# Projections: DMA queue order in the first, second and last batch, earlier mask rows, and one row product moved

## Chip, cores and metric

The kernel runs on one core of a Trainium2 chip. The metric is the device time of one execution in microseconds (us). An execution taken by the hardware profiler gives the trace that is read here. In it PE is TensorE (PEld its weight loads), DVE is VectorE, ACT is ScalarE, POOL is GpSimd and SP is SyncE, which here only issues DMAs.

## The reference, cut to what matters

A cross-attention block and a feed-forward block, 8 batches of 512 tokens with 512 features, 16 heads. The part that the change touches is the projection of queries, keys and values and what it prepares.

```python
q = split_heads(layernorm(x) @ Wq.T + bq)
k = split_heads(ctx @ Wk.T + bk)
v = split_heads(ctx @ Wv.T + bv)
scores = einsum('bhqd,bhkd->bhqk', q, k) / sqrt(32)
scores = where(mask == 0, -1e9, scores) + attn_bias
x = x + (einsum('bhqk,bhkd->bhqd', softmax(scores), v)) @ Wo.T + bo
x = x + feed_forward(layernorm(x))     # W1, gelu, W2, and a routed low-rank part
```

## The kernel before

The kernel has three blocks in a row: `project` makes q, k and v of all batches and stores them in DRAM, `attend` does the attention, `blend` the output projection and the feed-forward part. All engines end a block before the next begins. Within a block each engine runs a program of its own, written out by hand in `walk(engine, body)`, with one `body(b, more)` for each batch b; semaphores order them. So on each engine, and on SP's DMA queue, an instruction that waits holds all that stand behind it.

All products are of 32-bit numbers split into a high and a low half, three passes for each (`PASSES`). PE, for each batch: four key products (L797 on), four value products, four query products, of 12 matmuls with 512 columns each; each product ends in one of four PSUM banks of `ps_j`, which ACT (keys, `k_s`) or DVE (values `v_s`, queries `q_s`) must have evicted before the bank's next product starts. Between them stand the row products (`row_product`, L719): DVE makes diagonal matrices (`diagonal`, L501 on) of a per-token factor, and one matmul with ones turns them into a row over the tokens. R_HIGH and R_LOW are the two halves of 1/std of x; they are summed in one bank. FAC is 1 for a query row that has any allowed key. They stand after the first value product (R_HIGH), after the second or third (R_LOW), and at the end of the values (FAC); in batch 0 FAC stands behind the last query product. `keep_row` (L658) copies the R row on ACT, L692 the FAC row; DVE multiplies the queries by both (`scale_queries`, `mask_queries`).

DVE's order in a batch (L549 on): statistics of x, high half of 1/std with its diagonals, low half of xT (`p_xT_l`, L572), diagonals of R_LOW, first value tile, then the mask rows (L587 to L596): `pos` from the mask, its minimum over keys, and `q_fac` from it; the diagonals of FAC, the other values, the low half of the next context (`context_low`, L498), the queries. POOL makes 1/std (`root`, L435), four sums of a piece of the feed-forward weight W1 (`weight_sums`, L422 on) and the low halves of seven operands of it (L458). ACT makes the high halves (`feed_high`, L650), which wait for the load of the piece (`wf_in`) and for the sums. ACT does the piece of batch b at the end of batch b, that of batch 0 in batch 1. In the last batch POOL also makes three mask tiles for the attention (L405, L411, L417; 128x2048 each); the second waits for its bias load and for the last `p_xT_l`.

SP's queue (L314 to L367) in a batch: load the W1 piece (`load_ff`), next context, next x, store keys, next xT, store pos, next mask, store values, store queries, wait for `wf_low`, store the feed parts (`store_ff`, two DMAs of 896 KB). In batch 0 the two halves of Wo (`store_wo`, 1 MB each) and the W1 piece go out between mask and values. In the last batch the four query tiles are stored one by one; before the third SP waits for the feed parts, loads `late.pos` and stores the feed parts.

Of the kernel before, what the change touches and what calls it, by code (L numbers as in the profile page):

```python
# [20 lines left out]
I32 = mybir.dt.int32  # L21
ALU = mybir.AluOpType
ACT = mybir.ActivationFunctionType
AX_X = mybir.AxisListType.X
# [6 lines left out]
NC = D // P  # L31
# [9 lines left out]
MASKED = 1.0e9  # L41
# [83 lines left out]
def tokens(ap):  # L125

    return ap.rearrange("(t p) n -> p t n", p=P)
# [32 lines left out]
def project(nc, ident, ones, neg_half, x, xT, ctxT, mask, WqT, bq, WkT, bk, WvT, bv, W1T,  # L160
# [3 lines left out]
    with ExitStack() as ctx:  # L164
# [9 lines left out]
        c_raw, m_raw, pos = late.bias  # L174
# [5 lines left out]
        pos_min = sb("pos_min", [P, NT])  # L180
# [70 lines left out]
        def _(sp):  # L251
# [23 lines left out]
            def store_qk(b, src, dst, out):  # L275
                sp.dma_start(dst.rearrange("(c b) p n -> b p c n", c=NC)[b], src[:, :, :]).then_inc(out, 16)
# [10 lines left out]
            def store_wo():  # L287
                for n, part in enumerate((wf_h, wf_l)):
                    sp.dma_start(wo_d[n], part[:, :, :, :].rearrange("p f i n -> p (f i n)").bitcast(F32)) \
                        .then_inc(wo_out, 16)  # L290
# [21 lines left out]
                        sp.dma_start(ahead.k[:, n, :], k_d[n]).then_inc(ahead.qk_in[n], 16)  # L312

            def body(b, more):  # L314
                if b > 0:
                    sp.wait_ge(wf_low, 4 * b)
                    load_ff(b)
                if not more:
                    sp.wait_ge(cT_low, B - 1)
                    load_bias(1)  # L320
                if b >= B - 3:
                    load_ahead(b - (B - 3))
                if more:
                    need(sp, cT_low, b)
                    if b == 0:
                        sp.wait_ge(piece_low, 2 * NC)
                    load_c(b + 1)
                    sp.wait_ge(stats_done, NT * (b + 1))
                    load_x(b + 1)
                sp.wait_ge(k_done, NC * (b + 1))  # L330
                store_qk(b, k_s, k_d, k_out)
                if more:
                    sp.wait_ge(xT_low, NC * (b + 1))
                    load_xT(b + 1)
                sp.wait_ge(pos_done, b + 1)
                sp.dma_start(tokens(pos_d[b]), pos[:, :, :]).then_inc(pos_out, 16)
                if more:
                    load_m(b + 1)
                else:
                    load_bias(2)  # L340
                if b == 0:
                    sp.wait_ge(wo_low, 1)
                    store_wo()
                    load_ff(b)
                for t in range(0 if more else NT):
                    sp.wait_ge(bank_free, NPB + NVQ * b + t + 1)
                    sp.dma_start(tokens(v_d[b])[:, t, :], v_s[:, t, :]).then_inc(v_out, 16)
                    if t == 1:
                        sp.wait_ge(min_done, B)
                        sp.wait_ge(pos_out, 16 * (B + 1))  # L350
                        load_bias(3)
                sp.wait_ge(bank_free, NPB + NVQ * b + NT)
                if more:
                    sp.dma_start(tokens(v_d[b]), v_s[:, :, :]).then_inc(v_out, 16)
                if more:
                    sp.wait_ge(q_done, NC * (b + 1))
                    store_qk(b, q_s, q_d, q_out)
                else:
                    for c in range(NC):
                        if c == NC // 2:  # L360
                            load_more_pos()
                            store_ff(b)
                        sp.wait_ge(q_done, NC * b + c + 1)
                        sp.dma_start(q_d[B * c + b], q_s[:, c, :]).then_inc(q_out, 16)
                if more:
                    sp.wait_ge(wf_low, 4 * b + 4)
                    store_ff(b)  # L367

# [97 lines left out]
        def _(dve):  # L466
# [72 lines left out]
            def first_minima(j):  # L539
                for i in range(HG):  # L540
# [4 lines left out]
                                             late.tiles[j][:, i:i + 1, :], 1.0, 3.0e38, ALU.add, ALU.min,  # L545
                                             late.nmax[:, j, i:i + 1]).then_inc(late.summed, 1)

            def body(b, more):

                dve.wait_ge(x_in, 16 * b + 16)  # L550
# [16 lines left out]
                if b == 0:  # L567
                    weight_low(0)
                    add_weights()
                for c in range(NC):  # L570
                    dve.wait_ge(xT_high, NC * b + c + 1)
                    dve.tensor_tensor(out=xT_l[:, c, :], in0=xT_raw[:, c, :], in1=xT_h[:, c, :].bitcast(F32),  # L572
                                      op=ALU.subtract).then_inc(xT_low, 1)
# [7 lines left out]
                if b == 0:  # L581
# [2 lines left out]
                    values(b, 1, NT)  # L584
                    dve.wait_ge(w_low, 2 * NC)

                dve.wait_ge(m_in, 16 * b + 16)  # L587
                dve.wait_ge(pos_out, 16 * (b + 1))
                dve.tensor_scalar(pos[:, :, :], m_raw[:, :, :].bitcast(I32), 0.0, MASKED, ALU.is_equal, ALU.mult) \
                    .then_inc(pos_done, 1)  # L590
                dve.wait_ge(pos_done, b + 1)
                dve.tensor_reduce(pos_min[:, :], pos[:, :, :], AX_X, ALU.min).then_inc(min_done, 1)
                dve.wait_ge(min_done, b + 1)


                dve.tensor_scalar(q_fac[:, :], pos_min[:, :], 0.0, None, ALU.is_equal).then_inc(fac_done, 1)  # L596
                dve.wait_ge(fac_done, NFAC * b + FAC)
                dve.wait_ge(fac_turned, NFAC * b + R_LOW)
                diagonal(q_fac)
# [114 lines left out]
        def _(pe):  # L714
# [51 lines left out]
            def body(b, more):  # L766
# [14 lines left out]
                def features(w, a, c):  # L781
                    cs = slice(c * P, (c + 1) * P)
                    return [(w[m][:, k, cs], a[n][:, k, :]) for k in range(NC) for m, n in PASSES]

                need(pe, cT_low, b)
                if b == 0:
                    first_keys()
                else:
                    for c in range(NC):
                        product(K_AT + c, features((w_h[1], w_l[1]), (cT_h, cT_l), c))  # L790
                for t in range(NT):
                    ts = slice(t * P, (t + 1) * P)
                    product(V_AT + t, [(a[:, k, ts], w[:, k, :]) for k in range(NC)
                                       for a, w in ((cT_h, w_h[2]), (cT_h, w_l[2]), (cT_l, w_h[2]))])
                    if t == 0:
                        row_product(b, R_HIGH)
                    if b == 0 and t == 1:  # L797
                        weight_means()
                    if t == (1 if b else 2):
                        row_product(b, R_LOW)  # L800
                if b > 0:
                    row_product(b, FAC)
# [1 line left out]
                pe.wait_ge(xT_low, NC * (b + 1))  # L804
                for c in range(NC):
                    product(Q_AT + c, features((w_h[0], w_l[0]), (xT_h, xT_l), c))
                    if b == 0 and c == NC - 1:
                        row_product(b, FAC)
                    if not more and c == 0:
                        pe.wait_ge(ahead.qk_in[0], 32)  # L810
                        pe.wait_ge(fac_row_done, 2 * B)
                        scores(0)
                    if not more and c == 2:
                        pe.wait_ge(late.summed, HG)
                        scores(1)
# [1396 lines left out]
```

## Time and profile before

| | |
|---|---|
| median of 3 runs | 1797.74 us (1796.21 to 1799.68) |
| the profiled execution | 1796.49 us, span 1794.7 us |
| projections / attention from | 0 / about 299.7 us |
| PE busy over the span | 1763.7 us (98%) |
| DVE, ACT, POOL busy | 1271.9, 912.4, 972.3 us |
| chain that ended last | PE 50% (L2126 20%, L2100 17%, L1999 7%, L2038 5%), DVE 2% |
| DMA | 396.90 MB, mean 221 GB/s |

The time between the span and the execution is 1.8 us. PE's busy time is modelled and its instructions overlap, so that a full PE shows as 98%; what the projections lose has to be read from the timeline, instruction by instruction. A row of the timeline names start, duration, engine, line, operation, tiles, the number of merged instructions, and in brackets the idle time before it with what released it. An engine that waits inside an instruction (for a memory port) shows as busy.

### The profile page before, as it was taken

Reading aid. Unit: us, or ns where it says so; the run is one execution under the profiler, and the core shown is the slowest. Engines: PE = TensorE matmul, PEld = TensorE weight load, DVE = VectorE, ACT = ScalarE, POOL = GpSimd, SP = SyncE. Lnnn points to the kernel's source line nnn. Section 1 sums busy time; section 2 is a strip of 40 time slices with the busy share of each in tenths; the row PEclk is TensorE's granted clock in tenths of the full one; section 3 lists DMA queues with packets and bytes.
Section 4 is the critical chain, followed back from the end, with each engine's and each line's share of the span. In section 5 each row is a group of like instructions: output and inputs, shape, how many; then the busy total and the mean of one; then the engine's idle time right before and its main releaser. Section 6 shows DMA issues by size and latency. Waiting matters only on the chain.

```text
span 1794.7 us, 33910 instructions
## 1 busy us (share of the span) xinstructions
PE 1763.7 (98%) x11842; PEld 1359.1 (76%) x11842; DVE 1271.9 (71%) x2866; ACT 912.4 (51%) x2038; POOL 972.3 (54%) x466
## 2 busy tenths in 40 slices
PE   9899998999999999999999999999999999999999
PEld 7688885555555555555788888888988889888888
DVE  7677777999999999999757565455654556645553
ACT  4222324999999999999534242312423224222231
POOL 1423336999999999999446333233342333423321
PEclk9999998999999999999999999999999999999999
DMA  9799999636437245430479694865948669577584
GB/s 320 285 372 341 341 357 314 224 114 217 129 109 235 95 142 195 136 131 13 154 246 308 211 311 131 314 201 180 323 136 294 212 192 311 164 254 246 164 277 146
DMA packets 213079, 396.90 MB, mean 221 GB/s; under 512 B 15280, under 2 KB 54832, under 8 KB 212400
## 3 DMA queue, kind: packets, MB, share of 16 engines
q1 hardware_dynamic: 209360, 381.62, 63.2%
q0 software_dynamic: 3264, 12.58, 2.0%
q8 instruction: 98, 1.61, 0.4%
q10 hardware_dynamic: 288, 0.52, 0.1%
q14 instruction: 69, 0.57, 0.1%
HBM read 319.17 MB, written 75.50 MB: 220 GB/s over the span
## 4 chain that ended last, share of the span: by engine, by line
PE 50%; DVE 2%; issue 0%; POOL 0%; ACT 0%; DVEq 0%; ACTq 0%
PE banks L2126 20%; PE banks L2100 17%; PE banks L1999 7%; PE banks L2038 5%; PE banks L1993 1%; DVE k_x L1554 0%; DVE k_x L1725 0%; DVE h_q L1715 0%; DVE n_w L1652 0%; DVE n_ru_l L1540 0%; DVE n_stats L1561 0%; DVE n_zo L1547 0%; DVE n_sel L1660 0%; DVE n_g_h L1732 0%; DVE k_az L1577 0%
## 5 line engine op out<-in xcount | busy, mean ns | idle before, releaser
L2100 PEld LDWEIGHTS banks<-n_zo,n_w 128*128 128x128 f32 x2688 | 500.2, 188 | 66.3 <-DVE h_bias L1838 2.4
L2100 PE MATMUL banks<-n_zo,n_w 128*128 128x256 f32 x2688 | 533.4, 282 | 3.5 <-DVE h_bias L1838 2.2
L1483 POOL TENSOR_TENSOR n_g_l<-h_pos,n_g_h 128x512 fp32r<-128x512 f32 x128 | 196.2, 1533 | 558.9 <-DVE n_g_h L1732 558.9
L2126 PE MATMUL banks<-n_w,n_g_h 128*128 128x512 f32 x1024 | 383.7, 394 | 0.0
L1200 ACT ACTIVATE l_tiles<-l_tiles,l_small 128x512 f32<-128x512 f32 x376 | 267.3, 715 | 0.0
L1134 DVE CUSTOM_DVE_ANT_0 l_tiles<-banks,l_tiles 128x512 f32<-128x512 f32 x353 | 224.9, 687 | 24.6 <-PE banks L1036 23.8
L1047 PEld LDWEIGHTS banks<-ident,l_tiles 128*128 128x128 f32 x1524 | 164.8, 142 | 90.6 <-issue 72.8
L1047 PE MATMUL banks<-ident,l_tiles 128*128 128x128 f32 x1524 | 209.4, 281 | 0.7 <-ACT a_pT L1178 0.7
L2126 PE MATMUL banks<-n_w,n_g_l 128*128 128x512 f32 x512 | 201.9, 394 | 0.0
L2126 PEld LDWEIGHTS banks<-n_w,n_g_h 128*128 128x128 f32 x1024 | 193.4, 189 | 8.1
L1141 DVE COPY a_pT<-banks 128x512 f32<-128x512 f32 x256 | 164.5, 683 | 10.1 <-PE banks L1047 5.2
L1178 ACT ACTIVATE a_pT<-banks 128x512 f32<-128x512 f32 x256 | 151.5, 592 | 36.8 <-PE banks L1047 26.8
L1036 PE MATMUL banks<-h_k,h_q 32*128 32x512 f32 x1008 | 144.7, 643 | 8.1 <-PEq L164 6.3
L1061 PE MATMUL banks<-a_pT,a_v 128*32 128x256 f32 x2048 | 149.9, 388 | 0.0
L1001 POOL TENSOR_TENSOR l_tiles<-a_pos,l_bias 128x2048 f32<-128x2048 f32 (+1 forms) x32 | 137.3, 4299 | 4.2 <-PE banks L1047 4.1
L1971 ACT ACTIVATE h_pos<-h_pos 128x512 f32<-128x512 f32 x64 | 40.5, 632 | 192.4 <-DVE h_pos L1850 192.2
L1954 ACT ACTIVATE h_pos<-banks 128x256 f32<-128x256 f32 x64 | 24.6, 384 | 179.0 <-PE banks L2100 179.0
L1838 DVE TENSOR_TENSOR h_bias<-banks,h_bias 128x256 f32<-128x256 f32 x64 | 27.2, 424 | 113.6 <-PE banks L2100 113.5
L2126 PEld LDWEIGHTS banks<-n_w,n_g_l 128*128 128x128 f32 x512 | 96.5, 189 | 5.3
L1842 DVE TENSOR_TENSOR h_bias<-banks,h_bias 128x256 f32<-128x256 f32 x64 | 26.9, 420 | 100.9 <-PE banks L2100 100.9
L1200 ACT ACTIVATE a_t_s<-a_t_s,l_small 128x512 f32<-128x512 f32 x128 | 91.5, 720 | 0.0
L2038 PE MATMUL banks<-n_ru_h,n_zo 128*128 128x512 f32 x256 | 90.4, 392 | 0.0
(263 smaller groups left out, 3525.6 us busy)
## 6 DMA issues: line engine op xcount, KB each, us to landing
n_w<-wf_d SPq DMA_DIRECT2D x448, 256.0 KB, 3.6
n_w<-w_d SPq DMA_DIRECT2D x112, 512.0 KB, 4.5
a_pos<-pos_d SPq DMA_DIRECT2D x16, 1024.0 KB, 5.6
l_bias<-in_bias POOLq DMA_DIRECT2D x9, 1024.0 KB, 8.5
l_tiles<-in_x SPq DMA_DIRECT2D x8, 1024.0 KB, 10.1
l_tiles<-in_xT SPq DMA_DIRECT2D x8, 1024.0 KB, 12.9
l_bias<-in_mask SPq DMA_DIRECT2D x8, 1024.0 KB, 13.3
k_d<-l_tiles SPq DMA_DIRECT2D x8, 1024.0 KB, 11.5
```

What stands on the lines that cost most here:

```text
L1001: pool.tensor_tensor(out=t_s[j % NN][:, first:end, :], in0=pos_rows(b, qt, qt + 1).broadcast_to([P, end - first, S]), in1=bias_rows(first, ...
L1036: pe.matmul(ps_s[:, i, :], q[rows, b, qt * P:(qt + 1) * P], k[rows, b, :], start=True, stop=True).then_inc(scored, 1)
L1047: last = pe.transpose(ps_t[:, BANK[i], kt * P:(kt + 1) * P], t_s[at[1] % NN][:, i, kt * P:(kt + 1) * P], ident[:, :])
L1061: last = pe.matmul(ps_o[rows, :], v[:, b, kt, rows], pT[:, h, i, kt, :], start=kt == 0, stop=kt == NT - 1)
L1134: dve.tensor_tensor_reduce(t_s[j % NN][:, i:i + 1, :], ps_s[:, i:i + 1, :], added, 1.0, 3.0e38, ALU.add, ALU.min, nmax[:, j % NN, i:i + 1] ...
L1141: dve.tensor_copy(dst, src).then_inc(kept_dve, 1)
L1178: act.activation(dst, src, ACT.Copy).then_inc(kept_act, 1)
L1200: act.activation(t_s[j % NN][:, i, :], t_s[j % NN][:, i, :], ACT.Exp, scale=-1.0, bias=nmax[:, j % NN, i:i + 1], accum_out=total[:, j // 2 ...
L1483: pool.tensor_tensor(out=g_l[:, j % NG, :], in0=g_f[:, j % NG, :], in1=g_h[:, j % NG, :].bitcast(F32), op=ALU.subtract).then_inc(g_low, 1)
L2038: last = pe.matmul(ps_m[:, t % 2, :], z_tokens(i, c, t), ru[j][:, c, :], start=s == 0, stop=s == NRP - 1)
L2100: last = pe.matmul(bank, w1[:, q % NR, m, k * P:(k + 1) * P], zo[:, j, MOVING[i], k, :], start=s == 0 and i in (P1, P6, P5), stop=s == NPP ...
L2126: last = pe.matmul(ps_y[:, t, :], (g_h, g_l)[i][:, j % NG, t * P:(t + 1) * P], w2[:, j % NG, k, :], start=f == 0 and m == 0, stop=f == NF ...
```

## The change

Four edits, all in `project`.

1. SP, batches 0 and 1. `store_wo` moves from before the values of batch 0 to behind its query store. The store of the feed parts of batch 0 and the load of the W1 piece of batch 1, until now at the end of batch 0 and the start of batch 1, stand behind the value store of batch 1.
2. SP, last batch. The wait for the feed parts, the load of `late.pos` and the two feed stores stand before the second query tile instead of the third.
3. DVE. The mask rows become a function `mask_rows(b)`; from batch 1 on they are made before the low half of xT. In batch 0 they stay where they are.
4. PE. FAC of batch 0 moves behind the first key product of batch 1. R_LOW of batch 1 moves from after the second to after the third value product.

```diff
             def body(b, more):
-                if b > 0:
+                if b > 1:
                     sp.wait_ge(wf_low, 4 * b)
                     load_ff(b)
...
                 if b == 0:
                     sp.wait_ge(wo_low, 1)
-                    store_wo()
                     load_ff(b)
...
                 if more:
                     sp.dma_start(tokens(v_d[b]), v_s[:, :, :]).then_inc(v_out, 16)
+                if b == 1:
+                    sp.wait_ge(wf_low, 4)
+                    store_ff(0)
+                    load_ff(1)
                 if more:
                     sp.wait_ge(q_done, NC * (b + 1))
                     store_qk(b, q_s, q_d, q_out)
+                    if b == 0:
+                        store_wo()
                 else:
                     for c in range(NC):
-                        if c == NC // 2:
+                        if c == 1:
                             load_more_pos()
                             store_ff(b)
                         sp.wait_ge(q_done, NC * b + c + 1)
                         sp.dma_start(q_d[B * c + b], q_s[:, c, :]).then_inc(q_out, 16)
-                if more:
+                if more and b > 0:
                     sp.wait_ge(wf_low, 4 * b + 4)
                     store_ff(b)
...
+            def mask_rows(b):
+                dve.wait_ge(m_in, 16 * b + 16)
+                dve.wait_ge(pos_out, 16 * (b + 1))
...     # the lines of L587 to L596, moved
                 if b == 0:
                     weight_low(0)
                     add_weights()
+                else:
+                    mask_rows(b)
                 for c in range(NC):
                     dve.wait_ge(xT_high, NC * b + c + 1)
...
+                if b == 0:
+                    mask_rows(b)
                 dve.wait_ge(fac_done, NFAC * b + FAC)
...
                         product(K_AT + c, features((w_h[1], w_l[1]), (cT_h, cT_l), c))
+                        if b == 1 and c == 0:
+                            row_product(0, FAC)
...
-                    if t == (1 if b else 2):
+                    if t == (1 if b > 1 else 2):
                         row_product(b, R_LOW)
...
                     product(Q_AT + c, features((w_h[0], w_l[0]), (xT_h, xT_l), c))
-                    if b == 0 and c == NC - 1:
-                        row_product(b, FAC)
```

## Rows read from the trace of the kernel before

**Rows 1.** PE's timeline, rows with idle time before them: start, us, what, [idle <-releaser]

```profile
44.83 0.47 PE L778 MATMUL banks<-p_cT_h,p_wk_h 128*128 128x512 f32 x1 [1.15 <-DVE p_q_s L526]
...
68.18 0.51 PE L723 MATMUL banks<-p_fac_diag,p_ones_r 128*128 128x512 f32 x1 [0.85 <-DVE p_fac_diag L503]
...
85.49 0.77 PE L778 MATMUL banks<-p_cT_h,p_wk_h 128*128 128x512 f32 x1 [5.92 <-DVE p_q_s L526]
...
278.12 0.51 PE L723 MATMUL banks<-p_fac_diag,p_ones_r 128*128 128x512 f32 x1 [1.39 <-DVE p_fac_diag L503]
...
299.68 2.09 PE L1036 MATMUL banks<-h_k,h_q 32*128 32x512 f32 x8 [6.25 <-PEq L164]
```

**Rows 2.** PE's timeline, R_HIGH row products of batches 3 and 4

```profile
134.24 0.40 PE L723 MATMUL banks<-p_fac_diag,p_ones_r 128*128 128x512 f32 x1
...
167.62 0.40 PE L723 MATMUL banks<-p_fac_diag,p_ones_r 128*128 128x512 f32 x1
```

**Rows 3.** Waits of SP's queue, projections: engine, line <- releaser: total, times, longest

```profile
SPq L285 <- POOL p_wf_l L458: 16.6, 1, 16.6
```

**Rows 4.** SP's timeline, load of the context of batch 2

```profile
71.87 1.35 SPq L270 DMA_DIRECT2D l_bias<-in_ctxT  x1
```

**Rows 5.** ACT's timeline, batches 1 and 2: feed, context and xT copies

```profile
62.40 1.97 ACT L656 ACTIVATE p_wf_h<-l_pos 128x512 fp32r<-128x512 f32 x4
...
80.51 1.91 ACT L664 ACTIVATE p_cT_h<-l_bias 128x2048 fp32r<-128x2048 f32 x1 [16.14 <-DMA l_bias<-in_ctxT]
...
88.38 2.19 ACT L647 ACTIVATE p_xT_h<-l_tiles 128x512 fp32r<-128x512 f32 x4 [3.61 <-DMA l_tiles<-in_xT]
```

**Rows 6.** Stretch: us, busy of PE, PEld, DVE, ACT, POOL; clock, DMA share, GB/s

```profile
82.00:83.00 1.00, 0.00 (x0) 0.00 (x0) 0.55 (x1) 1.00 (x3) 0.00 (x0) 0.58 1.05 395
```

**Rows 7.** Two stretches with a full DMA queue, columns as in rows 6

```profile
94.00:97.00 3.00, 3.00 (x14) 2.46 (x14) 1.66 (x11) 0.69 (x1) 1.02 (x1) 1.00 1.04 401
119.50:153.00 33.50, 33.50 (x149) 27.71 (x148) 24.77 (x44) 9.81 (x15) 11.34 (x9) 1.00 1.03 366
```

**Rows 8.** DMA issues: near 256 the queries, near 69 W1T; last figure: us to landing

```profile
q_d<-p_q_s SPq DMA_DIRECT2D x1, 1024.0 KB, 4.9
...
l_pos<-in_W1T SPq DMA_DIRECT2D x2, 256.0 KB, 7.5
```

**Rows 9.** DVE's timeline: masking in batch 0; mask rows' start, then FAC diagonals

```profile
46.39 2.74 DVE L535 SCALAR_TENSOR_TENSOR p_q_s<-p_q_s,p_bq_c,p_fac_diag 128x512 f32<-128x512 f32 x4
...
137.12 1.21 DVE L589 TENSOR_SCALAR l_bias<-l_bias 128x2048 f32<-128x2048 int32 x1
...
140.90 0.87 DVE L503 TENSOR_SCALAR p_fac_diag<-ident,p_q_fac 128x128 fp32r<-128x128 f32 x4
```

**Rows 10.** POOL's timeline: root, low feed parts, first of four sums

```profile
52.32 1.01 POOL L435 TENSOR_TENSOR p_rstd<-p_var_e,neg_half 128x4 f32<-128x4 f32 x1 [14.96 <-DVE p_var_e L558]
...
63.17 4.48 POOL L458 TENSOR_TENSOR p_wf_l<-l_pos,p_wf_h 128x512 fp32r<-128x512 f32 x4 [3.44 <-ACT p_wf_h L656]
...
77.79 0.73 POOL L426 TENSOR_TENSOR l_pos<-l_pos 128x256 f32<-128x256 f32 x1 [10.14 <-DMA l_pos<-in_W1T]
```

**Rows 11.** DVE's timeline, last batch: low half of xT, R_LOW diagonals, q_fac

```profile
265.67 2.50 DVE L572 TENSOR_TENSOR p_xT_l<-l_tiles,p_xT_h 128x512 fp32r<-128x512 f32 x4
268.38 2.36 DVE L503 TENSOR_SCALAR p_fac_diag<-ident,l_small 128x128 fp32r<-128x128 f32 x4 [0.22 <-PE banks L723]
...
274.91 2.25 DVE L596 TENSOR_SCALAR p_q_fac<-p_pos_min 128x4 f32<-128x4 f32 x1
```

**Rows 12.** POOL's timeline, last batch: second mask tile

```profile
272.53 4.60 POOL L411 TENSOR_TENSOR l_tiles<-h_pos,l_bias 128x2048 f32<-128x2048 f32 x1 [1.05 <-issue]
```

**Rows 13.** SP's timeline, last batch: the four query stores

```profile
283.70 9.21 SPq L364 DMA_DIRECT2D q_d<-p_q_s  x2
...
294.75 4.17 SPq L364 DMA_DIRECT2D q_d<-p_q_s  x2
```

**Rows 14.** PE's timeline: the second group of eight score matmuls

```profile
307.19 1.24 PE L1036 MATMUL banks<-h_k,h_q 32*128 32x512 f32 x8
```

More of the change, by code:

```diff
@@ L546, in first_minima @@
                                              late.nmax[:, j, i:i + 1]).then_inc(late.summed, 1)
+            def mask_rows(b):
+                dve.wait_ge(m_in, 16 * b + 16)
+                dve.wait_ge(pos_out, 16 * (b + 1))
+                dve.tensor_scalar(pos[:, :, :], m_raw[:, :, :].bitcast(I32), 0.0, MASKED, ALU.is_equal, ALU.mult) \
+                    .then_inc(pos_done, 1)
+                dve.wait_ge(pos_done, b + 1)
+                dve.tensor_reduce(pos_min[:, :], pos[:, :, :], AX_X, ALU.min).then_inc(min_done, 1)
+                dve.wait_ge(min_done, b + 1)
+                dve.tensor_scalar(q_fac[:, :], pos_min[:, :], 0.0, None, ALU.is_equal).then_inc(fac_done, 1)
             def body(b, more):
@@ L585, in body @@
                     dve.wait_ge(w_low, 2 * NC)
[L587 to L596, printed above, removed]
+                if b == 0:
+                    mask_rows(b)
                 dve.wait_ge(fac_done, NFAC * b + FAC)
```

## Prediction, made before the changed kernel was run

> **What bounds the kernel now.** I read the page first: TensorE (PE) is busy for 98% of the span, so time can be won or lost only where PE stands still or runs at its lower clock. Then PE's timeline of the projections [rows 1]. It has five halts: 1.15 us at 44.83 (start of batch 1), 0.85 us at 68.18, 5.92 us at 85.49 (start of batch 2), 1.39 us at 278.12 (last batch), and 6.25 us at 299.68, where the attention block begins. The batches between have none: the same row product comes at 134.24 and 167.62 [rows 2], a period of 33.38 us. That is 12 products and 3 row products of 0.23, so a product is 2.72. I count from T, the start of a batch's first key product: the first row product (R_HIGH) is due at T+13.6, R_LOW at T+16.6 after the second value product, the third (FAC) at T+22.3. Batch 3 has T = 134.24 - 13.62 = 120.6. From 85.49 one period gives 118.9, so batch 2 lost a further 1.75 to the clock: it fell to 0.58 in the third microsecond of the halt [rows 6].
>
> The halt of 5.92 is put down to the vector engine (DVE). Read on: ScalarE (ACT) waited 16.14 us for the context of batch 2 and copied it at 80.51 [rows 5]; DVE then made its low part. Its load was issued at 71.87 [rows 4], because SP had stood 16.6 us before the store of the first feed part, for GpSimd's (POOL's) p_wf_l [rows 3]. That is the wait which the change moves.
>
> **Batches 0 to 2, part by part.** Context 2 now goes out right after the query and wo stores of batch 0, near 53, and the halts at 68.18 and 85.49 go. FAC of batch 0 costs PE 0.23 that the halt at 44.83 hid before. It also comes later: 44.83 + 2.72 = 47.6, about 0.4 to its end, ACT's copy 0.6, so DVE's masking of the queries starts at 48.7, not 46.39, and with its 2.74 [rows 9] ends at 51.4. The statistics of batch 1 and all behind them shift by 2.3. In batch 1 the mask rows (137.12 to 140.90 in batch 3, so 3.78 [rows 9]) stand before xT's low half. POOL's root moves from 52.32 to 54.6 [rows 10]; with its 1.0, the R_HIGH diagonals 1.2, the mask rows 3.8, xT_l 2.5 and the R_LOW diagonals 0.87 free [rows 9] this is 64.0, and about 65 since POOL's sums fall beside it. R_LOW, moved behind the third value product, is due at 44.8 + 0.3 + 7 products + 0.2 = 64.4, so I charge 0.6 (bounds 0 and 1.5). T of batch 2 becomes 44.83 + 33.38 + 0.1 + 0.23 + 0.6 = 79.2, against 85.49.
>
> What is late next? The feed load of batch 1 (W1T). SP issues it behind the value store, and the queue is now full ahead of it: from 51.4 it gets q, two wo halves, context 2, x 2, k, xT 2, pos, mask 2 and v, ten transfers of 1.05 MB; then two feed stores (1.84 MB) and the load (0.52 MB), 12.85 MB in all. Full queues moved 401 and 366 GB/s [rows 7]; I take 380, 33.8 us. A transfer into an almost empty queue landed 4.9 us after issue, of which 2.7 is its own data [rows 8], so 2.2 is overhead. The load lands at 51.4 + 2.2 + 33.8 = 87.4 (bounds 85.6 and 89.5), where the trace has 69 + 7.5, about 77 [rows 8]. Behind the wait of ACT's feed copy on it stand the query copies and key evictions of batch 2; behind POOL's sums stands the root for batch 2's row. The chain from the landing L:
> - POOL's four sums of about 0.73 [rows 10]: L+2.9. ACT's last two feed copies, half of 1.97 [rows 5]: L+3.9. The xT copies, 2.19 [rows 5]: L+6.1. A key eviction, about 0.7: L+6.8 = 94.2. The first value product is due at 79.2 + 10.9 = 90.1 and needs that bank: a halt of 4.1.
> - POOL's low feed parts, 4.48, from L+2.9: L+7.4. Root, 1.0 [rows 10]: L+8.4. Cast, subtraction and R_HIGH diagonals: L+9.6. Mask rows, 3.78, now in this chain: L+13.3. xT_l, 2.5 [rows 11]: L+15.8. R_LOW diagonals: L+16.7 = 104.1. R_LOW was due at 79.2 + 16.6 = 95.8.
> So PE is 8.3 late at R_LOW in all; the half-speed clock after the first halt lies inside this. T of batch 3 = 104.1 + 16.8 = 120.9, against 120.6. **The first halt's gain is given back: +0.3** (with L: -1.5 to +2.4). Were the load early, T would be 79.2 + 33.4 = 112.6, -8.0.
>
> **Middle batches.** xT_l ends near T+13.3 instead of T+9.5, still before the R_LOW diagonals can start (they wait for R_HIGH, T+14): nothing. Pos and mask go on the queue some us earlier than now, and a mask is loaded a whole batch ahead of its use. Zero.
>
> **Last batch.** T is 254.2. DVE's chain has less slack here: xT_l begins at 265.67 and the R_LOW diagonals at 268.38, taking 2.36 instead of 0.87 beside POOL's sums [rows 11]. POOL's second mask tile (128x2048, 4.60 us) starts at 272.53 [rows 12], when its bias has landed. While it ran, a DVE operation on 4 columns took 2.25 us and ended as the tile did, at 277.2 [rows 11], which made the 1.39 halt. With the mask rows ahead of it xT_l ends at 268.2 + 3.8 = 272.0 or later (beside POOL's sums nearer 273), the four diagonals would need until 273 or 274, and the tile takes the port in their midst. The last one waits for its end: 277.1 to 279. R_LOW, due at 270.8, comes near 279: a halt of 8.1, and 1.75 of low clock after it, less the 1.5 that went with the old halt: **+8.3**. If the diagonals slip through first, it is 3 - 1.5 = +1.5.
> The rule that I weigh: the Trainium skill, SBUF — State Buffer, "SBUF: two separate sides", says that VectorE and GpSimd share a port pair which one instruction holds to its end while the other fully blocks, whoever starts first. By that rule all hangs on which starts first, and the sum would be +1.5 if the diagonals all did.
>
> **End of the projections.** SP's last two query stores took 4.17 us to issue, 294.75 to 298.92, behind the pos load and feed stores that it had issued at 292.9 to 294.7 [rows 13]; PE starts again 0.76 after it. The change lets those go behind the first query store of 283.70, once POOL's last feed parts are made (FAC at 278.1, two copies and POOL's 4.5: about 285), so 7 us earlier, and the queue is nearly empty when the last queries come. SP then ends at 294.75 and 0.4 for the last one, 295.1: 3.85 less, with no other engine that works longer. PE's idle time falls to 2.4 us, shorter than the 2.6 after which the clock fell at 82 [rows 6]. In the trace eight score matmuls took 2.09 at 299.68 and 1.24 at 307.19 [rows 1, 14], and this first step took 7.5 us where I estimate 5.1 at full clock, DVE's minima included: 2.4 less. **Together -6.3** (-3.9 to -7). If PE is 8 us late in the last batch, this all moves with it. Nothing of attention or feed-forward is changed.
>
> **Sum.** +0.3 + 8.3 - 6.3 = +2.3 us. The profiled execution took 1796.5 (span 1794.7 and 1.8 around it), which gives 1798.8; the median of the runs is 1.25 above it, so I forecast **1800.0**. From no change a measurement of this kernel can tell about 0.2%, 3.6 us.
>
> **Rivals.**
> - A, the diagonals win the port in the last batch. For it: a few tenths of a microsecond in either engine's start decide. Against it: the tile is ready by 272.5 and the diagonals need the time up to 273. Last batch +1.5: 0.3 + 1.5 - 6.3 = -4.5, 1793.2.
> - B, the feed load of batch 1 is not late. For it: it is only 0.5 MB and all it needs is some 9 us earlier. Against: ten megabytes stand ahead of it, and no full stretch is faster than 401 GB/s. Batches 0 to 2 give -8.0: total -6.0 with the collision (1791.7), -12.8 without (1784.9), about 1789 between. The Trainium skill, DMA: Bandwidth & Descriptors, "Queues, rings and completion order", says that descriptors are taken in ring order on each engine but that completion is not first in, first out over transfers; by that a small load could finish somewhat ahead.
> - C, slower: the feed stores and load move slowly. The trace shows them landing at 77.8 after 67.7, 10.1 us for 2.36 MB, where 380 GB/s and 2.2 give 8.4. L is then 89.1, and if the second halt of batch 2 also drops the clock, 1.75 is added: 2.3 + 1.7 + 1.75 = +5.8, 1803.5. It decides once L passes 88.7. The Trainium skill, HBM Reference, "Specifications (TRN2)", has 358 GB/s for a core; by it the 12.85 MB would take 35.9 us and L would be 89.5, though the rows here are faster.
> - D, the edit at the end changes nothing since another wait holds the block: +6.3 on the forecast. SP's last row ends only 0.8 before the first score matmul, so I hold this for small.
>
> **Chances.** Forecast 0.40 (own range 1796 to 1804), A 0.17, B 0.19, C 0.19, D 0.05. Faster by over 0.2%: B 0.19, of A 0.11, of the forecast 0.02, 0.32. Slower: C 0.16, D 0.05, of the forecast 0.06, 0.27. Within 0.2%: 0.41. The range 1788 to 1806 leaves out half of B and the far ends of C and D.
>
> **What would show it.** PE's timeline: no halt near 79; halts near 90 (about 4 us, for ACT's key eviction) and near 102 (for DVE's fac_diag); batch 3's T near 121. ACT waits for W1T at about 87. In the last batch a halt of some 8 us before the second row product, with a diagonal that ends when POOL's tile ends. The last SP issues take 0.4 each and the idle time before the first score matmul is near 2.4, with full clock. No halt at 90 means that B holds and my reading of the queue is wrong; a last batch without a long halt means A.

## The result: 0.2 to 0.3% slower, with the mechanisms as forecast

The changed kernel took 1803.11 us (median of 10 runs, 1800.18 to 1804.63), the kernel before 1797.76 us (10 runs, 1795.66 to 1799.68). The ratio is 1.0031 with an interval of 1.0021 to 1.0041, so it is slower by more than the 0.2% that can be told from no change. The profiled execution took 1800.18 us, with a span of 1798.4 us, against 1796.49 and 1794.7 before. So the two traces differ by 3.7 us and the medians by 5.35 us: the trace of the changed kernel is of its shortest execution, and what the others lose beyond it has to be found too.

The changed file is 5 lines longer from SP's last part on (L369 here is L364 of before, L416 is L411, L508 is L503, L531 is L526) and 9 lines longer from ACT's part on (L684 is L675, L732 is L723, L787 is L778, L1045 is L1036); the low half of xT is L589, in place of L572.

PE's timeline of the changed kernel, the rows that answer to [rows 1, 2, 14] (start, us, engine, line, operation, and the idle time before it with what ended it):

```profile
44.88 0.47 PE L787 MATMUL banks<-p_cT_h,p_wk_h 128*128 128x512 f32 x1 [1.17 <-DVE p_q_s L531]
...
65.98 0.50 PE L732 MATMUL banks<-p_fac_diag,p_ones_r 128*128 128x512 f32 x1 [0.89 <-DVE p_fac_diag L508]
...
95.98 0.79 PE L787 MATMUL banks<-p_wv_h,p_cT_h 128*128 128x512 f32 x1 [4.76 <-ACT l_tiles L684]
...
105.52 0.50 PE L732 MATMUL banks<-p_fac_diag,p_ones_r 128*128 128x512 f32 x1 [1.43 <-DVE p_fac_diag L508]
...
136.06 0.40 PE L732 MATMUL banks<-p_fac_diag,p_ones_r 128*128 128x512 f32 x1
...
280.44 0.79 PE L732 MATMUL banks<-p_fac_diag,p_ones_r 128*128 128x512 f32 x1 [7.52 <-DVE p_fac_diag L508]
...
305.75 1.14 PE L1045 MATMUL banks<-h_k,h_q 32*128 32x512 f32 x8 [2.26 <-PEq L164]
310.70 1.14 PE L1045 MATMUL banks<-h_k,h_q 32*128 32x512 f32 x8
315.62 1.14 PE L1045 MATMUL banks<-h_k,h_q 32*128 32x512 f32 x8
```

The halt at the start of batch 2 (5.92 us at 85.49) is gone, and in its place stand 4.76 us at 95.98, which ACT's key eviction ended, and 1.43 us at 105.52, which the R_LOW diagonals ended. R_HIGH of batch 3 comes at 136.06, 1.8 later than in [rows 2]. The last batch has one halt of 7.52 us where it had 1.39. The idle time ahead of the attention shrank from 6.25 to 2.26, and the first two groups of score matmuls lie 4.95 us apart where [rows 1, 14] have 7.51.

What held batch 2 is in ACT's timeline:

```profile
89.12 0.94 ACT L665 ACTIVATE p_wf_h<-l_pos 128x512 fp32r<-128x512 f32 x2 [17.47 <-DMA l_pos<-in_W1T]
92.13 1.15 ACT L665 ACTIVATE p_wf_h<-l_pos 128x512 fp32r<-128x512 f32 x2 [2.07 <-POOL l_pos L436]
93.19 2.17 ACT L656 ACTIVATE p_xT_h<-l_tiles 128x512 fp32r<-128x512 f32 x4
95.27 2.39 ACT L684 ACTIVATE l_tiles<-banks,p_bk_c 128x512 f32<-128x512 f32 x4
```

ACT waited 17.47 us for the piece of W1 and only then came to the key evictions that PE needed. From the issue of batch 0's query store (51.7) to that landing the DMA queue moved 370 GB/s in the mean; only the first 1.3 us were nearly idle, with 129 GB/s, and behind them it was 378 GB/s (stretch: us, busy of PE, PEld, DVE, ACT, POOL, then clock, DMA share, GB/s):

```profile
51.70:89.10 37.40, 36.37 (x160) 29.47 (x159) 27.94 (x52) 6.51 (x10) 8.41 (x9) 1.00 1.02 370
```

What held the last batch is in the timelines of DVE and POOL. The four diagonals of R_LOW began at 275.29, the tile operation of POOL at 275.53. Two diagonals were through in the usual 0.28 us each; the third took 4.52 us and ended at 280.20, just behind the tile's end at 280.11, and the fourth came after it:

```profile
271.81 3.56 DVE L589 TENSOR_TENSOR p_xT_l<-l_tiles,p_xT_h 128x512 fp32r<-128x512 f32 x4
275.29 5.10 DVE L508 TENSOR_SCALAR p_fac_diag<-ident,l_small 128x128 fp32r<-128x128 f32 x4
```

```profile
275.68 4.52 DVE L508 TENSOR_SCALAR p_fac_diag<-ident,l_small 128x128 fp32r<-128x128 f32 x1
```

```profile
275.53 4.58 POOL L416 TENSOR_TENSOR l_tiles<-h_pos,l_bias 128x2048 f32<-128x2048 f32 x1 [1.32 <-DVE p_xT_l L589]
```

SP's last stores, which took 4.17 us for two in [rows 13], take 2.37 for three, since the pos load and the feed stores went out 7 us before them:

```profile
293.77 0.32 SPq L369 DMA_DIRECT2D q_d<-p_q_s  x1
294.88 0.37 SPq L298 DMA_DIRECT2D l_pos<-pos_d  x1
...
302.65 2.37 SPq L369 DMA_DIRECT2D q_d<-p_q_s  x3
```

The books of the two traces: batches 0 to 2 +1.8 (136.06 against 134.24). The middle batches add nothing: from R_HIGH of batch 3 to that of batch 7 it is 133.74 us against 133.64. PE's work of the last batch ends at 303.49 against 293.43, +10.1, so the last batch gives +8.2. The third group of scores comes at 315.62 against 311.87, +3.75, so the end gives -6.3: 4.0 of idle time and 2.3 of clock. Nothing behind that adds to it.

### The profile page after: what moved, and what is told of

The parts are those of the page before. It is cut to its first block, busy times and chain, and to the rows that moved or that the text cites. A ratio compares the mean times of both kernels' runs of the same rounds, so it can differ in the third digit from the quotient of the medians.

```text
span 1798.4 us, 33910 instructions
## 1 busy us (share of the span) xinstructions
PE 1761.9 (98%) x11842; PEld 1356.9 (75%) x11842; DVE 1273.0 (71%) x2866; ACT 911.9 (51%) x2038; POOL 966.9 (54%) x466
## 4 chain that ended last, share of the span: by engine, by line
PE 49%; DVE 2%; issue 0%; POOL 0%; ACT 0%; DVEq 0%; ACTq 0%
PE banks L2135 19%; PE banks L2109 17%; PE banks L2008 7%; PE banks L2047 5%; PE banks L2002 1%; DVE k_x L1563 0%; DVE k_x L1734 0%; DVE h_q L1724 0%; DVE n_w L1661 0%; DVE n_ru_l L1549 0%; DVE n_ru_l L1729 0%; DVE n_stats L1570 0%; DVE n_zo L1556 0%; DVE n_sel L1669 0%; DVE k_az L1586 0%
## 5 line engine op out<-in xcount | busy, mean ns | idle before, releaser
L1045 PE MATMUL banks<-h_k,h_q 32*128 32x512 f32 x1008 | 143.7, 639 | 4.1 <-PEq L164 2.3
```

What stands on the lines that cost most here:

```text
L1045: pe.matmul(ps_s[:, i, :], q[rows, b, qt * P:(qt + 1) * P], k[rows, b, :], start=True, stop=True).then_inc(scored, 1)
```

## Experiments

Each kernel ran on a chip beside the kernel before. To compare places in two traces I count from the first key product of batch 1 (44.88 in the changed kernel, 44.83 before), which shifts by some tenths from one execution to another. So counted, R_HIGH of batch 3 comes after 89.4 us before and after 91.2 in the changed kernel.

**e1_sp_last: the edit at the end alone, in the kernel before.**

```diff
-                        if c == NC // 2:
+                        if c == 1:
                             load_more_pos()
                             store_ff(b)
```

> The kernel before with the edit of the last batch on SP alone: late.pos and the feed stores go out before the second query store. Theory (SP's issue of the last two query stores is what ends the block): these issues take 0.4 us each, the idle time before the first score matmuls falls from 6.25 to about 2.3 us, the clock stays up there, and the kernel is 6.3 us faster than before (4.0 from the issue, 2.3 from the clock). Rival (the block's end waits for something else): the time is that of before.

Measured: 1790.44 us, ratio 0.9964 (0.9951 to 0.9976), 6.7 us less. PE's and SP's timelines:

```profile
296.17 1.14 PE L1036 MATMUL banks<-h_k,h_q 32*128 32x512 f32 x8 [2.26 <-PEq L164]
301.12 1.14 PE L1036 MATMUL banks<-h_k,h_q 32*128 32x512 f32 x8
```

```profile
293.08 2.37 SPq L364 DMA_DIRECT2D q_d<-p_q_s  x3
```

The idle time is 2.26 instead of 6.25 and the first step 4.95 instead of 7.51, as in the changed kernel. Rival D falls. This one moved condition is the best part of the change.

**e2_mask_late_last and e3_mask_late_all: the mask rows back in their old place, in the last batch alone and in all.**

```diff
-                else:
+                elif more:                # e3: the two lines are gone
                     mask_rows(b)
...
-                if b == 0:
+                if b == 0 or not more:    # e3: mask_rows(b) in every batch
                     mask_rows(b)
```

> The changed kernel, but in the last batch the mask rows stay behind the first value tile. Theory (in the last batch the mask rows push the R_LOW diagonals into POOL's second mask tile): the halt of 7.5 us before R_LOW goes, the old one of about 1.4 before FAC comes back, and the time falls by 8.2 us against the changed kernel, so about 3 below before. Rival (the halt has another cause, such as the later start of the batch): it stays, and the time stays at 5 above before.

> The changed kernel with the mask rows in their old place in every batch; queue order and row products as changed. Theory: the halt of 4.8 us before the first value product of batch 2 stays, since it hangs on the W1T load alone; R_LOW of batch 2 is ready 3.8 us earlier, so its halt goes; batch 3 starts 1 to 1.5 us earlier than in the changed kernel, and with the last batch's 8.2 the time is about 9.5 below the changed kernel, 4 below before. Rival (the mask rows take part in the first halt too): that halt shrinks as well.

Measured: e2 1792.83 us, 0.9974 (0.9965 to 0.9984); e3 1790.48 us, 0.9958 (0.9945 to 0.9972). Undoing the order in the last batch alone is worth some 10 us between medians, 2 more than the 8.2 of the traces; the nine executions of e2 lie between 1790.7 and 1795.7, and the traced one is the longest of them. PE's timeline of e2 has the old halt back and nothing else in the last batch:

```profile
282.00 0.51 PE L732 MATMUL banks<-p_fac_diag,p_ones_r 128*128 128x512 f32 x1 [1.38 <-DVE p_fac_diag L508]
```

In e3 PE's timeline of batches 1 and 2 has these halts, and none at R_LOW of batch 2:

```profile
70.29 0.50 PE L729 MATMUL banks<-p_fac_diag,p_ones_r 128*128 128x512 f32 x1 [1.98 <-DVE p_fac_diag L508]
...
95.94 0.50 PE L784 MATMUL banks<-p_wv_h,p_cT_h 128*128 128x512 f32 x1 [3.35 <-ACT l_tiles L681]
```

The FAC diagonals of batch 1 now came last, 1.98 us late; W1T landed when it had (ACT copied it at 89.06). R_HIGH of batch 3 comes after 88.7 us, 2.5 earlier than in the changed kernel: the mask rows' 3.7 us in the chain of batch 2 had cost that. So the early mask rows save about 1 us in batch 1, cost some 3.5 in batch 2 (2.5 for the two together), and 8 in the last.

**e4_feed_decoupled: nothing urgent behind the late load.** ACT copies the piece behind the key evictions of batch 2, and POOL makes the root ahead of the sums.

```diff
+                if b == 2:
+                    feed_high(1)          # ACT, behind the key evictions of batch 2
...
-                if b > 0:
+                if b > 1:
                     feed_high(b)
...
-                if b != 1:
+                if b == 0 or b > 2:
                     root(b)
+                if b == 1:
+                    root(2)               # POOL, ahead of weight_sums(1)
```

> The changed kernel, but nothing of batch 2 stands behind the late W1T load of batch 1: ACT makes the high feed parts of batch 1 behind the key evictions of batch 2, and POOL makes the root of batch 2 before the sums of batch 1. Theory (the load lands near 89 because of the ten megabytes ahead of it, and what it costs comes from ACT and POOL waiting for it in order): both halts of batch 2 go though the load is as late. Since SP then holds the context of batch 3 behind the feed stores, a new halt of about 3 us comes at the start of batch 3; the time is about 6 below the changed kernel. Rival (the halts come from xT or the bank evictions themselves): they stay and the time is unchanged.

Measured: 1796.86 us, 0.9999 (0.999 to 1.0007), 6.3 less than the changed kernel and no different from the kernel before. W1T landed at 88.7, as late as ever, but the halt of 4.76 is gone, so it was ACT's order behind the load that made it. I had not foreseen a smaller halt at R_LOW of batch 2. The late context of batch 3 I had, as a halt of about 3 us at the start of that batch; it came as 1.92 us at its R_LOW. PE's timeline and ACT's:

```profile
98.50 0.50 PE L736 MATMUL banks<-p_fac_diag,p_ones_r 128*128 128x512 f32 x1 [1.53 <-DVE p_fac_diag L510]
...
134.45 0.51 PE L736 MATMUL banks<-p_fac_diag,p_ones_r 128*128 128x512 f32 x1 [1.92 <-DVE p_fac_diag L510]
```

```profile
110.74 1.92 ACT L675 ACTIVATE p_cT_h<-l_bias 128x2048 fp32r<-128x2048 f32 x1 [11.10 <-DMA l_bias<-in_ctxT]
```

**e5_combined: e4, mask rows late in the last batch, and the context and x of batch 3 ahead of the second feed store and load.**

```diff
+                if b == 2:                # SP, behind the loads of batch 3's context and x
+                    sp.wait_ge(wf_low, 8)
+                    store_ff(1)
+                    load_ff(2)
```

> The decoupled feed of batch 1, the mask rows in their old place in the last batch, and on SP the context and x of batch 3 ahead of the feed stores of batch 1 and the load of batch 2. Theory: no halt in batch 2 and none at the start of batch 3, T of batch 3 near 113.7 (before: 120.6, changed: 122.5); old halt of 1.4 in the last batch; 2.3 us idle at the end of the block. About 13 us below before, near 1784.5. Rival (the queue is so full that each fixed halt comes back a batch later): batch 3 or 4 halts by some us, and the time is near 1790.

Measured: 1788.90 us, 0.9943 (0.993 to 0.9955), 4.4 above what I expected. PE's timeline and DVE's show why:

```profile
98.78 0.65 PE L740 MATMUL banks<-p_fac_diag,p_ones_r 128*128 128x512 f32 x1 [2.15 <-DVE p_fac_diag L514]
```

```profile
90.72 4.67 DVE L595 TENSOR_TENSOR p_xT_l<-l_tiles,p_xT_h 128x512 fp32r<-128x512 f32 x4
95.31 3.41 DVE L514 TENSOR_SCALAR p_fac_diag<-ident,l_small 128x128 fp32r<-128x128 f32 x4
```

The low half of xT took 4.67 us where it takes 2.5 free, and the diagonals 3.41 instead of 0.87, while POOL's sums and low feed parts, which had waited for the load, ran at the same time (89.35 to 98.45). In the changed kernel the late load had kept the two apart: the root stood behind the sums. PE stood 2.15 us and then ran at half clock.

**e9_combined_row_later: e5, and R_LOW of batch 2 behind the third value product.** The row product gets 2.7 us more, against the 2.15 that were missing.

```diff
-                    if t == (1 if b > 1 else 2):
+                    if t == (1 if b > 2 else 2):
```

> The combined kernel of the run before (feed of batch 1 decoupled, mask rows late in the last batch, context and x of batch 3 early) with R_LOW of batch 2, too, after the third value product. In the combined kernel the R_LOW diagonals of batch 2 ended at 98.7, since POOL's sums and low feed parts now fall beside xT's low half (4.67 us instead of 2.49) and the diagonals (3.41 instead of 0.87); a halt of 2.15 us and a fall of the clock followed. Theory: R_LOW is now due near 99.7, so both go, batch 3 starts 3 to 4 us earlier than there (T near 114), and the median falls from 1788.9 to about 1785.5. Rival (the halt only moves to FAC, whose diagonals come behind R_LOW): no gain.

Measured: 1784.43 us (1782.61 to 1786.87), ratio 0.9923 (0.991 to 0.9937). It beats both kernels, the one before by 13.9 us; I had expected about 1785.5. DVE's and PE's timelines:

```profile
90.39 4.68 DVE L595 TENSOR_TENSOR p_xT_l<-l_tiles,p_xT_h 128x512 fp32r<-128x512 f32 x4
95.00 3.46 DVE L514 TENSOR_SCALAR p_fac_diag<-ident,l_small 128x128 fp32r<-128x128 f32 x4
```

```profile
126.70 0.40 PE L740 MATMUL banks<-p_fac_diag,p_ones_r 128*128 128x512 f32 x1
...
270.66 0.50 PE L740 MATMUL banks<-p_fac_diag,p_ones_r 128*128 128x512 f32 x1 [1.39 <-DVE p_fac_diag L514]
...
288.23 1.14 PE L1053 MATMUL banks<-h_k,h_q 32*128 32x512 f32 x8 [2.25 <-PEq L164]
```

The collision is as long as in e5, but PE has no halt in batch 2, and the load that lands at 89.0 harms nobody. R_HIGH of batch 3 comes after 82.3 us, 7.1 less than before. With the 6.3 of the end that is 13.4 of the 13.9.

**e6_tile_later: POOL's second mask tile behind the low feed parts of the last batch.** If the tile makes the long halt, the halt goes down to what the chain of DVE needs without it.

```diff
                     weight_sums(b)
-                    second_mask_tile()
...
                 if not more:
+                    second_mask_tile()
                     third_mask_tiles()
```

> The changed kernel, but POOL makes the second mask tile of the last batch only behind the low feed parts; the mask rows stay early. Theory (the halt of 7.5 us is POOL's tile holding the port that the last R_LOW diagonals need): the four diagonals take about 0.9 us and end near 276, the halt before R_LOW is about 3 us and no clock is lost, 6.6 less up to there; at the end of the block the third tile may now block DVE's second minima, which gives back up to 4.6. Time 2 to 6.6 below the changed kernel. Rival (the early mask rows alone make the row late): the halt stays at 7.5.

Measured: 1802.16 us, 1.0024 (1.0015 to 1.0033): hardly less than the changed kernel. DVE's and PE's timelines:

```profile
276.25 0.86 DVE L508 TENSOR_SCALAR p_fac_diag<-ident,l_small 128x128 fp32r<-128x128 f32 x4
```

```profile
105.00 0.50 PE L732 MATMUL banks<-p_fac_diag,p_ones_r 128*128 128x512 f32 x1 [2.00 <-DVE p_fac_diag L508]
...
137.13 0.40 PE L732 MATMUL banks<-p_fac_diag,p_ones_r 128*128 128x512 f32 x1
...
277.17 0.80 PE L732 MATMUL banks<-p_fac_diag,p_ones_r 128*128 128x512 f32 x1 [3.20 <-DVE p_fac_diag L508]
...
305.10 2.09 PE L1045 MATMUL banks<-h_k,h_q 32*128 32x512 f32 x8 [4.16 <-PEq L164]
```

The cause is confirmed and the gain is lost elsewhere. The diagonals take 0.86 and the halt is 4.3 shorter. But 3.20 us still lost the clock, where I had expected it to stay up, and POOL, with two tiles of 4.6 us behind its feed parts, ended only at 301.4. Beside its last tile DVE took 3.15 us to mask two queries, where it takes 1.41 in the changed kernel, so the last query was ready at 304.0, 3.1 us behind PE's last work instead of 1.2:

```profile
299.50 3.15 DVE L540 SCALAR_TENSOR_TENSOR p_q_s<-p_q_s,p_bq_c,p_fac_diag 128x512 f32<-128x512 f32 x2
```

PE stood idle for 4.16 us instead of 2.26, with half clock behind it. I had expected the third tile to cost something at the end, but in DVE's minima. This execution also lost 1.5 us in batch 2: R_LOW halted for 2.00 and the clock fell, and R_HIGH of batch 3 comes after 92.7 us, not 91.2.

**e7_changed_again: the changed kernel once more.**

> The changed kernel again. Of its ten executions two took 1800.2 and 1801.0 at a mean clock of 0.996, the others about 1803 at 0.992; the one profiled was the fastest. Theory: in most executions the clock also falls at one more of the halts that this kernel has (2.3 us at the block's end, or 1.4 us before R_LOW of batch 2), which costs about 2.5 us more; a further profile may show which. Rival: the spread is spread out over the whole kernel, and no single place differs.

Measured: 1802.11 us (11 runs, 1799.24 to 1803.65), 1.002 (1.0011 to 1.0029). The profiled execution, 1799.95, is again one of the shorter ones, and its trace has the same halts to 0.1 us behind the start of batch 1: it does not show what the others lose.

**e8_fac_old: FAC of batch 0 in its old place.**

```diff
-                        if b == 1 and c == 0:
-                            row_product(0, FAC)
...
+                    if b == 0 and c == NC - 1:
+                        row_product(b, FAC)
```

> The changed kernel with the FAC row product of batch 0 back in its old place, behind the last query product of batch 0. Theory: the masking of batch 0's queries starts near 46.4 instead of 48.9, the query store and all nine megabytes behind it go 2.3 us earlier, and the W1T load of batch 1 lands near 87, so batch 3 starts about 2.3 us earlier and the kernel is 2.3 us below the changed one. Rival (the load's landing is set by the bytes in flight after xT's low half, not by the start of the queue): landing and time do not move.

Measured: 1800.07 us, 1.0014 (1.0004 to 1.0023), 2.0 less than e7 on the same chip; the two intervals overlap, so the trace has to carry the point. ACT's and PE's timelines:

```profile
86.27 0.94 ACT L665 ACTIVATE p_wf_h<-l_pos 128x512 fp32r<-128x512 f32 x2 [16.66 <-DMA l_pos<-in_W1T]
```

```profile
93.14 0.79 PE L787 MATMUL banks<-p_wv_h,p_cT_h 128*128 128x512 f32 x1 [3.96 <-ACT l_tiles L684]
...
102.68 0.50 PE L732 MATMUL banks<-p_fac_diag,p_ones_r 128*128 128x512 f32 x1 [0.84 <-DVE p_fac_diag L508]
...
277.44 0.80 PE L732 MATMUL banks<-p_fac_diag,p_ones_r 128*128 128x512 f32 x1 [7.39 <-DVE p_fac_diag L508]
...
303.42 1.77 PE L1045 MATMUL banks<-h_k,h_q 32*128 32x512 f32 x8 [2.25 <-PEq L164]
310.63 1.14 PE L1045 MATMUL banks<-h_k,h_q 32*128 32x512 f32 x8
```

With the query store of batch 0 issued earlier, W1T lands 2.85 us earlier, and both halts and the 0.89 us in batch 1 shrink or go: R_HIGH of batch 3 after 88.5 us, 2.6 less than in the changed kernel. So the delay that FAC's move gives the masking (2.3 us forecast, 2.4 measured from batch 1's start) came out again at the end of the queue. This execution also shows what the two traced ones of the changed kernel do not: after the same idle time (2.25) the first scores run at half clock and the second group comes 7.21 us later instead of 4.95, 2.3 us lost. From R_LOW of the last batch to the first scores it took 25.98 us, where the changed kernel's trace has 25.31: another 0.7.

**e10_wo_early: the two halves of Wo back to their old place in SP's queue.** It was to show that the landing of W1T is set by the bytes that stand ahead of it.

```diff
                     sp.wait_ge(wo_low, 1)
+                    store_wo()
                     load_ff(b)
...
-                    if b == 0:
-                        store_wo()
```

> The changed kernel with the two wo stores back in front of the W1T load of batch 0; all else as changed. 2.1 MB fewer then stand before the W1T load of batch 1. Theory (landing is set by the bytes ahead of it in a full queue): it lands 5.6 us earlier, at 83.5 instead of 89.1; the first value product of batch 2 starts without a halt (91.2), R_LOW is ready at 83.5 + 16.7 = 100.2, a halt of about 3 us; batch 3 starts at 117.0 to 118.7 instead of 122.5, the time falls by 4 to 5.5 against the changed kernel. Rival (a small load finds its way past the others, or its landing hangs on the time of its issue, 79 to 84): landing and time stay.

Measured: 1801.05 us, 1.0014 (1.0005 to 1.0023), 1 to 2 us less than the changed kernel, of 4 to 5.5 that I expected. W1T did land earlier (ACT's copy at 85.84), but by 3.3 us and not by 5.6, and the first halt fell to 2.17. From the query store's issue to the landing the queue moved 12.9 MB in 34.9 us, against 13.8 MB in 37.4 in the changed kernel: only 0.9 MB less, not 2.1. Moved ahead, the Wo halves delayed the value store instead (SP was held in its issue for 7.12 us, against 1.88), so part of these bytes still stood ahead of the query store. And from 69 to 70 us the queue had run low, at 154 GB/s against 410 in the changed kernel, so that bytes issued before then no longer counted. The load landed 10.2 us after its first issue in both kernels, so this run does not show the landing as the plain sum of the bytes ahead. SP's timeline and PE's:

```profile
42.47 7.12 SPq L354 DMA_DIRECT2D v_d<-p_v_s  x1
```

```profile
92.72 0.50 PE L786 MATMUL banks<-p_wv_h,p_cT_h 128*128 128x512 f32 x1 [2.17 <-ACT l_tiles L683]
...
102.31 0.79 PE L731 MATMUL banks<-p_fac_diag,p_ones_r 128*128 128x512 f32 x1 [3.59 <-DVE p_fac_diag L507]
...
135.56 0.40 PE L731 MATMUL banks<-p_fac_diag,p_ones_r 128*128 128x512 f32 x1
...
279.99 0.80 PE L731 MATMUL banks<-p_fac_diag,p_ones_r 128*128 128x512 f32 x1 [7.46 <-DVE p_fac_diag L507]
...
305.89 1.88 PE L1044 MATMUL banks<-h_k,h_q 32*128 32x512 f32 x8 [2.26 <-PEq L164]
313.13 1.14 PE L1044 MATMUL banks<-h_k,h_q 32*128 32x512 f32 x8
```

In this trace the halt only moved. In the changed kernel the clock fell during the halt that ends at 95.98 (0.84 of full in 93 to 94, 0.50 from there to 100), and the half-speed products ran while the diagonals were being made: R_LOW waited 1.43. Here the first halt was short, the clock stayed up, PE came sooner to R_LOW, waited 3.59 us there, and lost the clock behind it, where nothing covers it. R_LOW comes 2.5 us earlier (58.1 us from batch 1's start against 60.6), and R_HIGH of batch 3 after 91.4 us against 91.2: no gain in this execution, which is one of the longest of the eleven. The median is 1 to 2 us lower all the same; four executions at a mean clock of 0.997 took 1796.2 to 1799.5, and what they did in batch 2 no trace shows. The last batch and the start of the attention lose the clock as in e8 (25.90 and 7.24 us).

## Why the prediction was nearly right, and where it was off

The forecast was 1798.8 for the profiled execution and 1800.0 for the median; measured were 1800.18 and 1803.11. So the trace is 1.4 above its forecast, nearly all of it in batches 0 to 2, and the median 3.1, since the medians also lie further above the trace (2.9) than the 1.25 I had allowed. That the forecast median equals the profiled time is chance, and so is that the measured median lies at the number of rival C. Point by point:

- **Context 2 early, two halts gone: right.** No halt near 79 or at batch 2's start; e1, which keeps the old order there, has the halt of 5.9 at 85.71.
- **W1T lands late: right in kind, 1.7 us late in size** (89.1, forecast 87.4). This is the term that was mis-sized. The rate was right (378 GB/s behind the first 1.3 us), the overhead of 2.2 was too high by some 1.3, and the store began 0.3 later. What I had left out is the query store of batch 1, issued at 83.87, behind W1T: the stretch to 89.1 moved 13.8 MB, not 12.85, and in the 2.9 us after it only 0.1 MB more was moved. So nearly the whole megabyte behind the load had been moved when the load landed, 2.5 us of the queue's time. Rival C had the number 89.1 from a lower rate, which was not the cause. Rival B falls: although only 0.5 MB was asked for, it landed when the bytes ahead of it and nearly all of the store behind it had been moved.
- **The chain from the landing: right.** Key eviction L+6.8, measured 6.9; R_LOW L+16.7, measured 16.4.
- **Batch 1's 0.6 for R_LOW: 0.89.** Together batches 0 to 2 cost 1.8, not 0.3.
- **Middle batches zero: right**, 0.1 over four batches.
- **Last batch +8.3: measured +8.2**, through the collision as described. e2 shows the mask rows as the cause, e6 the tile. The Trainium skill, SBUF — State Buffer, "SBUF: two separate sides", makes the pair of ports a lock held to an instruction's end; the third diagonal, which ended at 280.20 where the tile ended at 280.11, agrees.
- **End -6.3: measured -6.3 in the trace**, 4.0 of idle time and 2.3 of clock, and 6.7 in the medians of e1. In most executions of the changed kernel the 2.3 of clock seem not to be won. The step that failed is the sentence that the idle time of 2.4, being shorter than the 2.6 after which the clock had fallen before, would leave the clock up. It is so in five traces (the changed kernel, e1, e4, e7, e9). In five others, all with 2.25 or 2.26 us idle, it fell at once or soon after: the second group of scores came 7.21 and 7.24 us behind the first in e8 and e10, and 6.35 to 6.45 behind it in e2, e3 and e5. Of the 21 executions of the changed kernel 15 have a mean granted clock of 0.992 or 0.993, like the traced ones of e8 and e10, and take 1800.8 to 1804.6 us; the other 6, the two traced ones among them, have 0.996 and take 1799.2 to 1802.1. The 2.3 and 0.7 of e8 in most executions would put the median 3.0 above the trace; it is 2.9 above in the first ten and 2.2 in e7. No trace of the changed kernel itself shows it, so this part is inferred.
- **Rival C's other half, the clock lost at the second halt of batch 2**, is in the traces of e2 (halt of 2.17; R_HIGH of batch 3 after 92.8 us, 1.6 more than in the changed kernel) but not in the changed kernel's two, with 1.43 and 1.42, although the landing lay past the 88.7 at which I had it begin. How often it happens in the others is open.

## To carry to other kernels

When a transfer is moved in a full queue, add up the bytes ahead of every load behind it, and those issued just behind the load as well, and then list what stands behind the wait for that load on each engine: the price was not the load's but that of the evictions and the root queued behind it. When a step is moved on VectorE, look at what GpSimd does at its new time, and at the slack of every batch, since batches 3 to 6 hid the mask rows, batch 2 paid some 3.5 us for them and the last one 8. A halt that is shortened may only move to the next wait, and what it is worth depends on where the clock then falls; so take out the next waiter as well (e9), or expect little (e6, e10).

## What the runs showed of the hardware

- Halts of almost the same length ended with the clock up or down. At the start of the attention an idle time of 2.25 to 2.29 us left it up in five traces and not in five, at a price of 1.4 (e3) to 2.3 us (e8 and e10). In batches 1 to 3 halts of 1.43, 1.53, 1.92 and 1.98 left it up (changed kernel, e4, e4, e3) and those of 2.00, 2.15 and 2.17 at R_LOW did not (e6, e5, e2), but the one of 2.17 at the key eviction of e10 did. Such a halt has two prices, and a forecast should carry both.
- Four operations of DVE on 512 columns with two inputs in SBUF took 4.67 us beside POOL's sums and low feed parts (e5) against 2.49 without them (changed kernel, batch 2), the single ones between 0.68 and 1.78. Four diagonals took 3.41 against 0.87, the single ones between 0.28 and 1.32. POOL's own operations stretched as well: four low feed parts took 5.35 us against 4.40.
- Two loads of 256 KB in a full queue landed 7.7 and 6.9 us after their issues, the second one 10.2 us after the first issue began (78.93 in SP's timeline, landed 89.1). For 4.90 us of that SP itself was held in the two issues, where it takes 0.4 us for a store in an empty queue (51.66):

```profile
78.93 4.90 SPq L280 DMA_DIRECT2D l_pos<-in_W1T  x2
```
